# A graph layer with a top-k FFN on one core: the FFN on the chosen rows alone

## The reference

```
xn = layernorm(x)                                  # x: 3125 rows of 256, 53125 edges
x  = x + gnn(xn, edges) + mix(xn)                  # three graph layers: 1024, 512, 256 wide
n  = layernorm(x)
w  = n @ wr + br                                   # one router weight a row
sel = the 1561 rows with the largest w             # k = 1562, k - 1 are used
y[sel] = (gelu(n[sel] @ w1 + b1) @ w2 + b2) * w[sel]   # 256 -> 1024 -> 256
x  = x + y + n                                     # y is zero elsewhere
```

## Time and profile before

| | us |
|---|---|
| median of three runs (range) | 1459.4 (1458.06 to 1460.7) |
| the profiled execution's own time | 1460.05 |
| its span, first to last instruction | 1458.2 |
| mean granted clock of PE | 0.959 of 2.4 GHz |
| busy: PE, DVE, ACT, POOL | 1283.3, 821.0, 524.8, 530.6 |

### The profile page before, as it was taken

The page is one execution under the profiler, slowest core; times in us unless marked ns, Lnnn a source line. Parts: engine busy times, 40 slices in busy tenths (PEclk is TensorE's granted clock), DMA queues, the critical chain, the costliest instruction groups (busy, mean ns, idle before and its releaser), DMA issues.

```text
span 1458.2 us, 20220 instructions
## 1 busy us (share of the span) xinstructions
PE 1283.3 (88%) x7100; PEld 866.5 (59%) x7100; DVE 821.0 (56%) x1478; ACT 524.8 (36%) x984; POOL 530.6 (36%) x542
## 2 busy tenths in 40 slices
PE   1996776897679999999999999999999999778985
PEld 1763453654446666666665666666666555457775
DVE  6566677868745545454553222222222998878675
ACT  3323626458532222222221232222221212248952
POOL 1003777777767777776000000000004840223000
PEclk9988888998879999999999999999999999989998
DMA  9860000000323232222210422212222444110002
GB/s 270 285 228 1 1 1 1 1 1 1 90 69 82 52 76 50 75 61 65 72 43 24 121 65 65 64 46 62 64 64 66 131 126 129 44 44 1 1 1 88
DMA packets 46192, 99.52 MB, mean 68 GB/s; under 512 B 19079, under 2 KB 31252, under 8 KB 46002
## 3 DMA queue, kind: packets, MB, share of 16 engines
q1 hardware_dynamic: 32814, 98.55, 23.8%
q0 software_dynamic: 13312, 0.13, 0.7%
HBM read 75.79 MB, written 22.85 MB: 68 GB/s over the span
## 4 chain that ended last, share of the span: by engine, by line
PE 66%; DVE 20%; ACT 5%; issue 5%; DMA 1%; POOL 1%; SPq 0%; DVEq 0%; ACTq 0%; POOLq 0%
PE psum L1705 63%; DVE scr L1216 4%; DVE scr L948 3%; PE psum L2066 1%; DVE scr L1174 1%; ACT scr L1367 1%; POOL acc L571 1%; DVE scr L1167 1%; DVE big L1151 1%; DVE scr L1178 1%; DMA rows<-in_x 1%; DVE scr L1164 1%; DVE scr L1161 1%; DVE acc L1233 1%; PE psum L2044 1%
## 5 line engine op out<-in xcount | busy, mean ns | idle before, releaser
L550 POOL DMA_INDIRECT counts<-big,eidx x416 | 422.7, 1016 | 252.7 <-issue 130.9
L1705 PE MATMUL psum<-rows,scr 125*125 125x512 f16 x1250 | 278.3, 381 | 11.5 <-DVE scr L1164 9.3
L1705 PE MATMUL psum<-big,scr 125*125 125x512 f16 x1250 | 278.5, 379 | 1.0 <-DVE big L1068 1.0
L1705 PEld LDWEIGHTS psum<-rows,scr 125*125 125x125 f16 x1250 | 170.4, 137 | 113.3 <-DVE scr L1164 10.0
L1705 PEld LDWEIGHTS psum<-big,scr 125*125 125x125 f16 x1250 | 169.9, 137 | 95.2 <-DVE big L1068 1.5
L566 POOL MEMSET big<- 128x4 f16 x1 | 0.1, 115 | 422.1 <-PE psum L1705 422.1
L1705 PE MATMUL psum<-wb,scr 128*125 128x512 f16 x600 | 137.5, 379 | 1.4 <-DVE scr L1051 1.4
L1032 DVE TENSOR_SCALAR scr<-psum,col 125x256 f32<-125x256 f32 x25 | 12.1, 485 | 172.1 <-PE psum L1705 172.1
L1705 PEld LDWEIGHTS psum<-wb,scr 128*125 128x125 f16 x600 | 81.1, 136 | 45.8 <-DVE scr L1051 1.9
L1705 PE MATMUL psum<-big,wm 128*128 128x313 f32 x312 | 95.0, 455 | 12.3 <-ACT big L1420 7.2
L1705 PE MATMUL psum<-wb,big 128*125 128x256 f16 x600 | 75.7, 280 | 23.8 <-DVE big L1227 21.1
(11 more groups left out here) (367 smaller groups left out, 1909.1 us busy)
## 6 DMA issues: line engine op xcount, KB each, us to landing
scr<-counts SPq DMA_DIRECT2D x75, 683.6 KB
counts<-wb SPq DMA_DIRECT2D x25, 683.6 KB
counts<-big,eidx POOLq DMA_INDIRECT x416
scr<-counts SPq DMA_DIRECT2D x75, 79.3 KB
scr<-in_x SPq DMA_DIRECT2D x25, 125.0 KB
rows<-in_x SPq DMA_DIRECT2D x5, 560.0 KB
out<-acc SPq DMA_DIRECT2D x5, 560.0 KB
wb<-in_w SPq DMA_DIRECT2D x1, 2048.0 KB, 10.6
```

What stands on the lines that cost most here:

```text
L550: pool.indirect_dma_start(cells, bass.IndirectOffsetOnAxis(ap=eidx[:, r * EQ + g:r * EQ + g + 1], axis=0), evalue[:, at_c:at_c + 1], None, ...
L1705: return pe.matmul(o, l, r, start=start, stop=stop)
```

## The change

A search finds the threshold before the FFN starts, and the FFN runs on 13 tiles of 122 slots (SL) that hold the chosen rows, in chunks of 4, 5 and 4 tiles.

- Search: DVE compares all weights with 31 levels at once (63 in the last round), PE sums the comparisons over partitions, DVE adds up and takes the next digit of the float's bit pattern; six rounds, each waiting for the one before. Then each chosen row gets a slot number (sums over partitions with `tri` and `ones` on PE, a scan on DVE), and 25 one-hot matmuls turn that into a list of row indices (`picked`, and `picked_w` for the weights' order in DRAM).
- Rows: SP stores the normalised rows to DRAM during layer 3 (`store_staged`), and after it the weights and the base rows (sum plus normalised row, which ACT now makes in `base_row`) of all 25 tiles to `out`. POOL then issues 13 gathers of the chosen rows, 26 of their weights and base rows, and 13 scatters of finished rows into `out` as they come.
- FFN: PE turns the gathered rows in f32, ACT and DVE make both halves from PSUM. `take_y` now also scales and adds the base row, tile by tile.
- Bias sums: POOL's wait for the end of layer 2 ahead of them is gone, they follow the mix sums at the end of layer 1. The norms of the FFN's weights, their scales and POOL's weight halves come after tile 8 of layer 2.
- `stage_rows`, `count_above`, `wall`, `finish` and the late selection chain are gone. PE's one-time semaphores become one counter (`pe_milestones`).

The core of the diff. Left out are the new buffers, the renamed semaphores, and the middle of the slot chain (some twenty DVE ops of 25 elements, four of 25 x 13).

```diff
-ACT_COUNTS = 7
-COUNTED = 4
+KSEL = N // 2 - 1
+SL = 122
+CHUNKS = (4, 5, 4)
+SLOTS = sum(CHUNKS)
+LAST = KSEL - (SLOTS - 1) * SL
+FAR = 40
+SEARCH = ((26, 31), (21, 31), (16, 31), (11, 31), (6, 31), (0, 63))
+TG = 5
...
+        pd = picked_dram.rearrange("(t p) e -> p t e", p=P)
+
+        def store_staged(c):
+            sp.wait_ge(sem("xn2_done"), c * G + G)
+            for lo, hi in PARTS_OF_ROWS:
+                sp.dma_start(pd[lo:hi, c * G:(c + 1) * G, :], xn2[lo:hi, c * G:(c + 1) * G, :]).then_inc(
+                    sem("rows_stored"), 16)
 
...
+            if layer == 2:
+                for t in range(HEAD, T):
+                    sp.wait_ge(sem("agg_done"), base + t - RING + 1)
+                    fetch(t, (base + t) % RING)
+                    if t in (9, 14, 19, 24):
+                        store_staged((t - 9) // G)
...
-        sp.wait_ge(milestone("router_done"), AFTER["router_done"])
-        sp.wait_ge(sem("agg_done"), 3 * T)
-        sp.dma_start(w_dram.rearrange("(p t) -> p t", t=T), wv).then_inc(sem("w_stored"), 16)
-        sp.wait_ge(sem("w_stored"), 16)
-        load_rows(wall, bass.AP(w_dram.tensor, 0, [[0, P], [1, N]]), "wall_loaded")
+        store_staged(NC - 1)
+        sp.wait_ge(sem("w_done"), T)
+        sp.dma_start(w_dram.rearrange("(p t) -> p t", t=T), wv).then_inc(sem("rows_stored"), 16)
         od = out.rearrange("(t p) d -> p t d", p=P)
         with sp.Fori(0, NC) as i:
-            sp.wait_ge(sem("final_done"), i * G + G)
+            sp.wait_ge(sem("sum_done"), i * G + G)
             for lo, hi in PARTS_OF_ROWS:
                 sp.dma_start(od[lo:hi, bass.ds(i * G, G), :], accv[lo:hi, bass.ds(i * G, G), :]).then_inc(
-                    sem("stored"), 16)
-        sp.wait_ge(sem("stored"), ROWS_IN * NC)
+                    sem("base_stored"), 16)
+        sp.wait_ge(sem("base_stored"), ROWS_IN * NC)
...
-        def stage_rows(c):
-
-            pool.wait_ge(sem("xn2_done"), c * G + G)
-            if c >= 2:
-                pool.wait_ge(sem("tr_done"), 3 * c - 3)
-            done.did(pool.tensor_scalar(stage, xn2[:, c * G:c * G + G, :], NORMED, None, ALU.mult))
-            done.settle()
-            done.did(pool.tensor_copy(stage16[c % 2][:, 0], stage))
-            done.settle()
-            pool.tensor_tensor(stage16[c % 2][:, 1], stage, stage16[c % 2][:, 0], ALU.subtract).then_inc(
-                sem("stage_done"), 1)
-            pool.wait_ge(sem("stage_done"), c + 1)
-
-            pool.wait_ge(sem("sum_done"), c * G + G)
-            chunk = accv[:, c * G:c * G + G, :]
-            pool.tensor_tensor(chunk, chunk, xn2[:, c * G:c * G + G, :], ALU.add).then_inc(sem("xn2_added"), 1)
+        pool.wait_ge(sem("lo2_done"), T)
+        pool.wait_ge(sem("agg_done"), 2 * T)
+        pool.iota(counted, pattern=[[1, 63]], base=1, channel_multiplier=0,
+                  allow_small_or_imprecise_dtypes=True).then_inc(sem("search_ready"), 1)
...
+        pool.wait_ge(sem("rows_stored"), ROWS_IN * NC + 16)
+        pool.wait_ge(sem("picked_ready"), 1)
+        for g in range(SLOTS):
+            pool.indirect_dma_start(got[:, g, :], None, picked_dram,
+                                    bass.IndirectOffsetOnAxis(ap=picked[:, g:g + 1], axis=0),
+                                    bounds_check=N - 1, oob_is_err=False).then_inc(sem(f"got{chunk_of(g)}"), 16)
+        pool.wait_ge(sem("picked_ready"), 2)
+        pool.wait_ge(sem("base_stored"), ROWS_IN * NC)
+        w_cells = w_dram.rearrange("(n o) -> n o", o=1)
+        for g in range(SLOTS):
+            pool.indirect_dma_start(wgot[:, g:g + 1], None, w_cells,
+                                    bass.IndirectOffsetOnAxis(ap=picked_w[:, g:g + 1], axis=0),
+                                    bounds_check=N - 1, oob_is_err=False).then_inc(sem(f"beside{chunk_of(g)}"), 16)
+            pool.indirect_dma_start(base[:, g, :], None, out,
+                                    bass.IndirectOffsetOnAxis(ap=picked[:, g:g + 1], axis=0),
+                                    bounds_check=N - 1, oob_is_err=False).then_inc(sem(f"beside{chunk_of(g)}"), 16)
+        for c, tiles in enumerate(CHUNKS):
+            pool.wait_ge(sem(f"beside{c}"), 32 * tiles)
+        for g in range(SLOTS):
+            n = SL if g < SLOTS - 1 else LAST
+            pool.wait_ge(sem("final_done"), g + 1)
+            pool.indirect_dma_start(out, bass.IndirectOffsetOnAxis(ap=picked[:n, g:g + 1], axis=0),
+                                    base[:n, g, :], None, bounds_check=N - 1, oob_is_err=False).then_inc(
+                sem("stored"), 16)
+        pool.wait_ge(sem("stored"), 16 * SLOTS)
...
-        for t in range(HEAD):
+        for t in range(HEAD + RING):
             step2(t, t % 2, first=t == 0)
...
+        with dve.Fori(1, LOOPS) as i:
...
-            done.did(dve.reciprocal(rs4, root4))
-            done.settle()
+            dve.reciprocal(rs4, root4).then_inc(sem("rs4_done"), 1)
+            dve.wait_ge(sem("rs4_done"), t + 1)
...
+        dve.wait_ge(sem("search_ready"), 5)
+        for (shift, k), table in zip(SEARCH, tables):
+            done.did(dve.tensor_scalar(table, counted[:, 0:k], float(1 << shift), None, ALU.mult))
+        done.settle()
...
+        dve.wait_ge(sem("agg_done"), 3 * T)
+        done.did(dve.tensor_scalar(wfull, wv, brc[:, 0:1], None, ALU.add))
+        done.settle()
+        done.did(dve.tensor_scalar(junk63[:, 0:T], wfull, 0.0, None, ALU.is_gt))
+        done.settle()
+        dve.tensor_reduce(enough, junk63[:, 0:T], AX, ALU.add).then_inc(milestone("router_done"), 1)
+        dve.wait_ge(sem("answered"), 1)
+        done.did(dve.tensor_scalar(enough, bank(7, P, 1), float(KSEL), None, ALU.is_ge))
+        done.settle()
+        done.did(dve.tensor_scalar(sign, enough, 2.0, -1.0, ALU.mult, ALU.add))
+        done.did(dve.tensor_scalar(wanted, enough, float(2 * KSEL - N - 1), float(N - KSEL + 1), ALU.mult, ALU.add))
+        done.settle()
+        done.did(dve.tensor_scalar(signed, wfull, sign, None, ALU.mult))
+        done.settle()
+        for r, (shift, k) in enumerate(SEARCH):
+            levels = tables[0].bitcast(F32) if r == 0 else level[:, 0:k]
+            dve.tensor_tensor(compared[:, 0:T * k].rearrange("p (t k) -> p t k", t=T),
+                              free(signed, 0, [[1, T], [0, k]]), free(levels, 0, [[0, T], [1, k]]),
+                              ALU.is_ge).then_inc(sem("asked"), 1)
+            dve.wait_ge(sem("answered"), r + 2)
+            done.did(dve.tensor_reduce(counted[:, 0:k], free(bank(7, P, TG * k), 0, [[1, k], [k, TG]]), AX, ALU.add))
+            done.settle()
+            done.did(dve.tensor_scalar(junk63[:, 0:k], counted[:, 0:k], wanted, None, ALU.is_ge))
+            done.settle()
+            done.did(dve.tensor_reduce(digit, junk63[:, 0:k], AX, ALU.add))
+            done.settle()
+            done.did(dve.tensor_scalar(place.bitcast(I32), digit, float(1 << shift), None, ALU.mult))
+            done.settle()
+            done.did(dve.tensor_tensor(prefix.bitcast(I32), prefix.bitcast(I32), place.bitcast(I32), ALU.bitwise_or))
+            done.settle()
+            if r + 1 < len(SEARCH):
+                done.did(dve.tensor_tensor(level[:, 0:SEARCH[r + 1][1]].bitcast(I32), tables[r + 1],
+                                           free(prefix.bitcast(I32), 0, [[0, SEARCH[r + 1][1]]]), ALU.bitwise_or))
+                done.settle()
+        done.did(dve.tensor_tensor(limit, prefix, sign, ALU.mult))
+        done.settle()
+        dve.tensor_scalar(masks[:, 0, :], wfull, limit, None, ALU.is_gt).then_inc(sem("asked"), 1)
+        dve.tensor_scalar(masks[:, 1, :], wfull, limit, None, ALU.is_equal).then_inc(sem("asked"), 1)
+        done.did(dve.memset(fits, 0.0))
+        dve.wait_ge(sem("answered"), len(SEARCH) + 2)
...
+        for lo, hi in ((0, 7), (7, PAIRS)):
+            dve.tensor_tensor(ohb[:, lo:hi], free(row16, 2 * lo, [[2, hi - lo], [0, SL], [1, 2]]),
+                              free(iop_all[:P].bitcast(BF16), 0, [[0, hi - lo], [2, SL], [1, 2]]),
+                              ALU.is_equal).then_inc(sem("asked"), 1)
+        dve.wait_ge(sem("answered"), len(SEARCH) + 3)
+        done.did(dve.tensor_scalar(tile_of[:SL, 0:SLOTS], bank(7, SL, SLOTS), float(P), None, ALU.mult))
+        done.settle()
+        dve.tensor_tensor(picked, tile_of[:SL, 0:SLOTS], bank(7, SL, SLOTS, SLOTS), ALU.add).then_inc(
+            sem("picked_ready"), 1)
...
+        def take_y(c, j):
+            g = first_slot[c] + j
+            dve.wait_ge(sem("ypart_done"), c * 8 + 8)
+            dve.scalar_tensor_tensor(out=ytemp[:, j, :], in0=accumulator(j), scalar=out_back[:SL],
+                                     in1=fb2r_slots, op0=ALU.mult, op1=ALU.add).then_inc(sem("yffn_evac"), 1)
+            dve.wait_ge(sem("yffn_evac"), g + 1)
+            if j == 0:
+                dve.wait_ge(sem(f"beside{c}"), 32 * CHUNKS[c])
+                s, e = first_slot[c], first_slot[c] + CHUNKS[c]
```

(97 more changed lines are left out.)

387 lines of the change are left out of this document (178 added, 209 removed).

## The result

| | before | changed |
|---|---|---|
| median time, us (4 runs each) | 1460.05 (1458.06 to 1464.49) | 1421.99 (1421.83 to 1422.33) |
| ratio | | 0.973, interval 0.972 to 0.975 |
| profiled execution: time, span, us | 1460.05, 1458.2 | 1422.33, 1420.3 |

The change takes 38 us off. The forecast was 1398 with a range to 1419: the sign is right, and the gain of 62 us was too large by 24, which puts the time 3 us outside the range.

What follows compares the result with a forecast made beforehand. PE bounds the kernel. 62 us less: 21 from layer 3, 42 from FFN and end's 177 us becoming 35 search + 12 gather and turn + 78 + 10; 1395.6 plus 1.85 outside gives 1397.5, range 1386 to 1419.

Steps and rivals of the forecast that it cites:

- last aggregate ends: Layer 3: 23 tiles of 5.42 us on PE bring the last aggregate to 1253.0, before 1267.8.
- search: Before the FFN: start, six compare-and-sum rounds and places on DVE and PE take 35.1 us, bounds 28 and 50.
- picks to first turn: Ahead of the FFN: four gathers issued in 5.1 us plus a landing of 3.7 make 8.8, to 1304.2.
- FFN on PE: 13 tiles of 122: 66.6 us of matmuls plus turning, lower clock, chunk switches and waits make 78, bounds 72 and 86.
- tail: After PE: last scatter starts at 5.1 us, ends issuing at 6.1, lands 3.5 later; 9.9 with the end.
- layer 2's stall: POOL's weight pieces overlap two to three layer 2 tiles and may stretch DVE's ops: 0.5 us, bounds 0 and 6.
- nothing in sum: Layer 2: the two norms' matmuls (1.17 us of PE) stand after tile 8 instead of its end, at no net cost.
- Rival (d): Layer 3 bound by DVE through the base row, or layer 2's PE stalled by POOL: +5 to +12, 1406, chance 0.08.
- Rival (c): The search costs half as much again, PE at its low clock and handovers of 0.3: 50 us, 1413, chance 0.10.
- the price of an indirect transfer: POOL's FFN gathers and scatters: one every 1.27 us, as for two-byte scatters; a gather lands in 2.5 + 1.25.
- rival (a): FFN: few DMA engines per transfer: +1.9 us first chunk, +4.0 tail, 1404, chance 0.30; all sharing two: 1426, chance 0.05.
- rival (b): POOL's queue of 52 transfers bounds the end: pitch 1.8 to 3, 1400 to 1455, chance 0.04; 3.3, 1477, 0.03.

Runs made afterwards that it cites:

- e8: The kernel before with only bias sums, norms and weight halves moved into layer 2; ratio 0.9973 (0.9949 to 0.9997).
- e9: The kernel of e8 again, against the kernel before; ratio 0.9975 (0.9962 to 0.9988).
- e5: The changed kernel (122 rows) plus a small POOL memset marking the end of its last wait; span 1940.1 us, on chips some 520 us slower.
- e1: The changed kernel with tiles of 112 slots in place of 122, 14 tiles in chunks of 4, 5, 5; 1407.24 us, ratio 0.9638.

## Why the prediction was wrong, step by step

| step | forecast | measured | off by |
|---|---|---|---|
| last aggregate ends | 1253.0 | 1255.6 | +2.6 |
| to the last router weight | 7.3 | 7.5 | +0.2 |
| search | 35.1 | 34.2 | -0.9 |
| picks to first turn | 8.8 | 13.8 | +5.0 |
| turn and halve | 3.0 | 2.9 | -0.1 |
| FFN on PE | 78 | 83.7 | +5.7 |
| tail | 9.9 | 22.6 | +12.7 |
| layer 2's stall | 0.5 | 0 | -0.5 |

**Layers 1 to 3: held.** Layer 2 shows no stall of PE. DVE's tile stayed under PE's; the base row's cover gave out by 0.3 to 0.4 us a tile (DVE's wait for ACT at L1281) without reaching PE. Of the 2.6, 1.9 are there already at the start of layer 1 (428.36 us against 426.46), before any work that the change moves, and 1.0 is a step that I had put at "nothing in sum": the norms' matmuls had covered the wait at the head of layer 3, and their move leaves it open (1115.93, and the same in e8 and e9). Rival (d) did not happen.

**Search: held**, by its unit prices: compares of 0.97 and 1.80, rounds of 3.35 for 3.6, five matmuls 0.83 for 1.0. (By the rates given for wide operations the last compare comes to 1.76, not 1.80; that it was met to the hundredth is luck.) Rival (c) did not happen.

**The step that failed is the price of an indirect transfer**: "I take 1.27 and 2.5 + 1.25". Measured are a pitch of 2.03 us and, for the fourth gather, 4.8 where 2.5 + 1.25 stood (its issue ends at 1306.39, the turn starts at 1311.19), with 1.07 us from picks to first gather that I had not priced. The rows that it was read from, are of 128 partitions. I had written the few engines down as rival (a), from the share of 5 engines in the earlier trace rows, but charged them to the movement of bytes only, +1.9 and +4.0. The second of these was right: 3.5 + 4.0 is the 7.5 that the 97 rows take to land in e5. That few engines lengthen the issue as well was in no term. A pitch of 2.03 is past the 1.8 at which rival (b) puts POOL in charge. So what came is (b)'s middle form, to which I gave 0.04, by (a)'s cause, to which I gave 0.35: two rivals priced as separate cases were one. (b)'s formula gives 1295.4 + 52 x 2.03 + 7.5 = 1408.5 for the span, 11.8 short of the 1420.3. Its two landings, 7.5 together, were 5.5 (the wait for the last base rows, 1379 to 1385) and 8.9 (behind the last issue); the first gather started 3.1 later, and some transfers took longer than 2.03, nearly 2 us in all.

e1 undoes this one step and the time falls to 1407, 14.8 us less. Between the spans of the two traces (14.1) the parts are 7.0 at the first turn, 0.6 in PE's stretch and 6.5 behind PE. The measured table, issue in us, gathers and in brackets scatters; a landing counts from the start of the issue, one of a last scatter from its end:

| rows | largest divisor up to 16 | rows to a share | issue | landing |
|---|---|---|---|---|
| 96, last | 16 | 6 | (0.93) | 5.4 behind the issue, held by the scatter ahead |
| 112 | 16 | 7 | 0.99 (0.94) | median 2.7 |
| 105, last | 15 | 7 | (0.99) | 1.6 behind the issue |
| 124 | 4 | 31 | 1.38 (1.32) | median 4.3 |
| 122 | 2 | 61 | 1.73 (1.67) | median 5.4 |
| 73, last | 1 | 73 | (1.83) | not marked |
| 97, last | 1 | 97 | (2.16) | 7.5 behind the issue |

The issue of a scatter grows with the rows to a share from the first row of the table to the last. An estimate of it, from these rows alone: 0.85 us and 0.0135 for each row of a share, within 0.06 of every one.

The Trainium skill, "DMA: Bandwidth & Descriptors", section on why a DMA increments its semaphore by 16, has the rule of the second column, for queues fed by POOL too. The packets here agree with it (16, 15, 4, 2 and 1 shares for 112, 105, 124, 122 and 97 rows), and so do the landings.

**FFN on PE: pitches right, ends wrong.** 12 inner and 12 outer matmuls are 1.25 and 1.31 us apart as worked out, 15 outer 1.64. The 5.7 are: the lower clock, which took 2.3 and 1.7 us of the first two groups of 24 (4.98 and 4.33 us, where two groups of 12 otherwise take 2 x 1.25 and the 0.16 of overlap, 2.7) and 1.3 at 1380.48 (2.79 for 1.47), 5.3 for the 2.7 forecast; chunk switches of 2.49 and 3.85 for 4.8; a turn wait of 2.21 for 1.4; 0.8 is spread. The granted clock is 0.50, the lower of its two levels (1.2 GHz of 2.4), over 1298 to 1314 us, where PE waits for the gathers. It is 0.52 in the mean of 1314 to 1319, and 0.55 over 1380 to 1383, behind the wait of 3.85.

**Tail.** Forecast as one scatter behind DVE's last op. DVE's last op ends at 1402.55, as late behind PE as forecast (4.8 for 4.5), but POOL still had scatters to issue up to 1411.44. The step also put what comes after the landing at 0.3 us (9.6 became 9.9); it is 1.4 with 122 rows and 6.2 with 112. So even at the cheap transfer of e1 the tail is 16.1.

## What to carry to other kernels

Before pricing a transfer by another of its kind, compare the row counts by their divisors up to 16: 112 rows in 16 shares beat 122 in two, though they need one more tile of work. When two rivals share a cause, price them together: a price per item counts once for the first item, once for the queue and once for the last. And when work is moved out of a place, ask what wait it covered there.
